# Edge products of a graph attention kernel multiplied by x over four PSUM banks: two operations of 2048 elements a tile in place of four of 1024, and the weighing in one operation

## The reference

```
w_m = (efeat @ W_msg + b_msg).reshape(E, in_f, -1)
w_a = (efeat @ W_attn + b_attn).reshape(E, in_f, -1)
h_src = feat[src][:, :, None]
e1 = w_m * h_src
e2 = w_a * h_src
seg_max = jax.ops.segment_max(e2, dst, num_segments=N)
ex = jnp.exp(e2 - seg_max[dst])
denom = jax.ops.segment_sum(ex, dst, num_segments=N)
attn = ex / denom[dst]
ft = jax.ops.segment_sum(e1 * attn, dst, num_segments=N)
return layernorm(x + ft.sum(axis=1))
```

## Time and profile before

| | us |
|---|---|
| runs of the kernel, median (3 runs) | 1687.11 |
| lowest and highest | 1686.28, 1688.92 |
| the profiled execution's own time | 1689.2 |
| its span in the profile | 1687.1 |
| busy: PE, VectorE | 1308.6, 1514.4 |
| busy: ACT, POOL | 987.8, 966.8 |

### The profile page before, as it was taken

The page is one execution under the profiler, slowest core; times in us unless marked ns, Lnnn a source line. Parts: engine busy times, 40 slices in busy tenths (PEclk is TensorE's granted clock), DMA queues, the critical chain, the costliest instruction groups (busy, mean ns, idle before and its releaser), DMA issues. The chain is left out here.

```text
span 1687.1 us, 20610 instructions
## 1 busy us (share of the span) xinstructions
PE 1308.6 (78%) x5657; PEld 675.5 (40%) x5657; DVE 1514.4 (90%) x1504; ACT 987.8 (59%) x2062; POOL 966.8 (57%) x878
## 2 busy tenths in 40 slices
PE   0002799999999999999999999999999999998300
PEld 0001444444444444444444444444444444443200
DVE  8623899999999999999999999999999999998368
ACT  1002567767767767777777677677676666664100
POOL 5777777777676767677677777676770000000170
PEclk9999899999999999999999999999999999999655
DMA  4314344444444444444444444444443223221250
GB/s 109 81 19 106 89 131 122 128 128 118 133 125 115 132 126 119 128 125 119 130 122 124 129 118 131 125 116 133 125 118 115 88 79 99 84 75 51 62 149 15
DMA packets 175870, 182.93 MB, mean 108 GB/s; under 512 B 48376, under 2 KB 131208, under 8 KB 175758
## 3 DMA queue, kind: packets, MB, share of 16 engines
q1 hardware_dynamic: 141838, 158.74, 30.0%
q0 software_dynamic: 33920, 22.89, 9.5%
HBM read 92.36 MB, written 89.41 MB: 108 GB/s over the span
## 5 line engine op out<-in xcount | busy, mean ns | idle before, releaser
L490 POOL DMA_INDIRECT split<-x_parts,edge_src x784 | 873.1, 1114 | 321.5 <-issue 221.6
L797 PE MATMUL bank_sum<-em,row_onehot 128*128 128x512 f32 x1760 | 861.6, 602 | 31.0 <-ACT sum_rows L661 31.0
L1031 DVE TENSOR_TENSOR em<-bank_prod,h_rows 128x1024 f32<-128x1024 f32 x440 | 515.7, 1213 | 41.8 <-issue 32.6
L797 PEld LDWEIGHTS bank_sum<-em,row_onehot 128*128 128x128 f32 x1760 | 307.5, 189 | 269.4 <-issue 235.2
L1049 DVE TENSOR_TENSOR em<-em 128x1024 f32<-128x1024 f32 x220 | 267.8, 1218 | 3.5 <-ACT em L620 3.5
L785 PE MATMUL bank_prod<-w_rows,partsT 100*128 100x512 bf16 x880 | 269.5, 388 | 1.5 <-DVE em L1031 1.5
L1074 DVE TENSOR_TENSOR em<-em,bank_max 128x2048 f32<-128x2048 f32 x110 | 250.7, 2279 | 3.2 <-ACT node_max L652 3.2
L661 ACT COPY sum_rows<-bank_sum 128x512 f32<-128x512 f32 x220 | 126.6, 576 | 176.6 <-PE bank_sum L797 176.6
L620 ACT ACTIVATE em<-em 128x2048 f32<-128x2048 f32 x110 | 210.5, 1913 | 1.5 <-DVE em L1074 1.4
L644 ACT COPY chunk_fwd<-bank_max 128x512 f32<-128x512 f32 x110 | 64.5, 586 | 238.0 <-PE bank_max L727 238.0
L490 POOL DMA_INDIRECT em<-sums,rec_from_i x4 | 4.0, 992 | 305.2 <-DMA sums<-sum_rows 304.3
(11 more groups left out here) (166 smaller groups left out, 1214.6 us busy)
## 6 DMA issues: line engine op xcount, KB each, us to landing
sums<-sum_rows SPq DMA_DIRECT2D x110, 512.0 KB, 3.0
rec<-split_records SPq DMA_DIRECT2D x220, 144.0 KB, 2.2
split_records<-split SPq DMA_DIRECT2D x97, 288.0 KB
mask<-tile_table SPq DMA_DIRECT2D x110, 192.0 KB, 3.3
split<-x_parts,edge_src POOLq DMA_INDIRECT x784
rel<-tile_table SPq DMA_DIRECT2D x110, 64.0 KB, 3.0
edge_feat<-in_features SPq DMA_DIRECT2D x97, 64.0 KB
flag<-tile_table SPq DMA_DIRECT2D x110, 2.0 KB
```

What stands on the lines that cost most here:

```text
L490: return nc.gpsimd.indirect_dma_start(out, None, src, bass.IndirectOffsetOnAxis(idx, 0))
L797: mm = nc.tensor.matmul(bank_sum[:, :], row_onehot[:, t % RING, g, :], em[:, t % RING, s * GROUPS + g, :, :, :].rearrange("p i m o -> p (i ...
L1031: V.tensor_tensor(em[:, v, 2 * j:2 * j + 2, :, :, :].rearrange("p s i m o -> p s i (m o)"), bank_prod[j % 2][:, :, :].rearrange("p s (i x) ...
```

## The change

The four PSUM banks of the products become one tensor, `bank_four`. `products` has two halves of four matmuls each in place of four pairs. Each half writes all four banks, and waits until the multiplication of the half before it has ended. `times_features` has two halves of 2048 elements. For that, `h_rows` is laid out by set and not by group, and ACT's copy writes it so. `weigh` takes all eight sets at once. The waits on `prod_ready`, `times_h` and `weighted` count accordingly.

```diff
-        h_rows = sb("h_rows", [P, 2, GROUPS, SLOTS * FEAT])
+        h_rows = sb("h_rows", [P, 2, SLOTS, GROUPS, FEAT])
...
-        bank_prod = [ps(f"bank_prod{i}", [P, 2, BOTH]) for i in range(2)]
+        bank_four = ps("bank_four", [P, 4, BOTH])
+        bank_prod = [bank_four[:, 0:2, :], bank_four[:, 2:4, :]]
...
-                since(act, times_h, 4 * (t - 1))
-                nc.scalar.copy(h_rows[:, t % 2, :, :].rearrange("p g k -> p (g k)"),
-                               bank_t[0][:, 0:GROUPS * SLOTS * FEAT]).then_inc(h_copied, 1)
+                since(act, times_h, 2 * (t - 1))
+                nc.scalar.copy(h_rows[:, t % 2, :, :, :].rearrange("p s g k -> p g s k"),
+                               bank_t[0][:, 0:GROUPS * SLOTS * FEAT].rearrange("p (g s k) -> p g s k", g=GROUPS, s=SLOTS)
+                               ).then_inc(h_copied, 1)
...
-                since(pe, times_h, 4 * t + j - 1)
-                for g in range(GROUPS):
-                    k = GROUPS * j + g
-                    mm = nc.tensor.matmul(bank_prod[j % 2][:, g, :], partsT[:, t % 2, k * P:(k + 1) * P],
+                since(pe, times_h, 2 * t + half)
+                for k in range(SIDE // 2):
+                    at = half * SIDE // 2 + k
+                    mm = nc.tensor.matmul(bank_four[:, k, :], partsT[:, t % 2, at * P:(at + 1) * P],
                                           w_rows[:, :], start=True, stop=True)
...
                 sum_slots(t - 2, 0, [0])
-                products(t + 1, 2)
                 give_features(t + 2)
-                products(t + 1, 3)
-                sum_slots(t - 2, 0, [1])
-                sum_slots(t - 2, 0, [2])
+                products(t + 1, 1)
+                sum_slots(t - 2, 0, [1, 2])
                 turn_back(t)
                 sum_slots(t - 2, 0, [3])
-                products(t + 2, 0)
                 pick_ends(t)
                 sum_slots(t - 2, 1, [0])
-                products(t + 2, 1)
+                products(t + 2, 0)
                 sum_slots(t - 2, 1, [1, 2, 3])
...
-                v_eng.wait_ge(prod_ready, 4 * t + j + 1)
-                h = h_rows[:, t % 2, :, FEAT * j:FEAT * (j + 1)]
-                V.tensor_tensor(em[:, v, 2 * j:2 * j + 2, :, :, :].rearrange("p s i m o -> p s i (m o)"),
-                                bank_prod[j % 2][:, :, :].rearrange("p s (i x) -> p s i x", i=FEAT),
-                                bc(h, 3, [P, GROUPS, FEAT, 2 * FEAT]), ALU.mult).then_inc(times_h, 1)
+                v_eng.wait_ge(prod_ready, 2 * t + half + 1)
+                h = h_rows[:, t % 2, 2 * half:2 * half + 2, :, :].rearrange("p s g k -> p (s g k)")
+                n = SIDE // 2 * FEAT
+                V.tensor_tensor(em[:, v, 4 * half:4 * half + 4, :, :, :].rearrange("p s i m o -> p (s i) (m o)"),
+                                bank_four[:, :, :].rearrange("p s (i x) -> p (s i) x", i=FEAT),
+                                bc(h, 2, [P, n, 2 * FEAT]), ALU.mult).then_inc(times_h, 1)
```

More of the change, by code:

```diff
@@ L422, in load_flags @@
                 since(sp, h_ready, t - 1)
-                since(sp, prod_ready, 4 * (t - 1))
+                since(sp, prod_ready, 2 * (t - 1))
                 sp.dma_start(flag8[:, w, :], tab_d[t:t + 1, 4 * WIDE:8 * WIDE].rearrange("t (k c) -> (t k) c", k=SIDE)
@@ L624, in copy_parts @@
                     return
-                since(act, prod_ready, 4 * (t - 1))
+                since(act, prod_ready, 2 * (t - 1))
                 for half in range(2):
@@ L774, in give_features, with products @@
                 mm.then_inc(h_ready, 1)
-            def products(t, j):
+            def products(t, half):
                 if not tile(t):
                     return
-                if j == 0:
+                if half == 0:
                     pe.wait_ge(t_copied, 2 * (t + 1))
                     pe.wait_ge(flags_landed[t % 2], 2 * rounds(t, 2))
-                since(pe, times_h, 4 * t + j - 1)
-                for g in range(GROUPS):
-                    k = GROUPS * j + g
-                    mm = nc.tensor.matmul(bank_prod[j % 2][:, g, :], partsT[:, t % 2, k * P:(k + 1) * P],
+                since(pe, times_h, 2 * t + half)
+                for k in range(SIDE // 2):
+                    at = half * SIDE // 2 + k
+                    mm = nc.tensor.matmul(bank_four[:, k, :], partsT[:, t % 2, at * P:(at + 1) * P],
                                           w_rows[:, :], start=True, stop=True)
@@ L792, in sum_slots @@
                 if slots[0] == 0:
-                    pe.wait_ge(weighted, 2 * (t + 1))
+                    pe.wait_ge(weighted, t + 1)
                     pe.wait_ge(onehot_ready, 2 * (t + 1))
@@ L1019, in _, with times_features @@
             v_eng.wait_ge(chunk_ready, 2)
-            def times_features(t, j):
+            def times_features(t, half):
                 if not tile(t):
@@ L1042, in run_forward, with weigh @@
                                      ALU.max).then_inc(fwd_done, 1)
-            def weigh(t, half):
+            def weigh(t):
                 if not tile(t):
@@ L1047, in weigh @@
                 v_eng.wait_ge(exp_done, t + 1)
-                m = em[:, t % RING, 4 * half:4 * half + 4, :, 1, :]
-                V.tensor_tensor(m, m, em[:, t % RING, 4 * half:4 * half + 4, :, 0, :], ALU.mult).then_inc(weighted, 1)
+                m = em[:, t % RING, :, :, 1, :]
+                V.tensor_tensor(m, m, em[:, t % RING, :, :, 0, :], ALU.mult).then_inc(weighted, 1)
             def max_slots(t):
@@ L1054, in max_slots @@
                 v = t % RING
-                v_eng.wait_ge(times_h, 4 * (t + 1))
+                v_eng.wait_ge(times_h, 2 * (t + 1))
                 V.tensor_tensor(max4[:, :, :, :], em[:, v, 0:4, :, 0, :], em[:, v, 4:8, :, 0, :],
@@ L1078, in _ @@
                 times_features(t + 1, 0)
+                run_forward(t)
+                weigh(t - 1)
                 times_features(t + 1, 1)
[L1080 to L1083, removed]
                 max_slots(t + 1)
-                weigh(t - 1, 1)
                 max_chunks(t + 1)
```

## The result

| | us |
|---|---|
| the changed kernel, median (4 runs) | 1779.15 |
| lowest and highest | 1777.65, 1779.79 |
| the kernel before beside it, median (4 runs) | 1687.94 |
| span in the profile, changed and before | 1777.2, 1687.1 |

The ratio is 1.054, with a 95% interval from 1.0522 to 1.0558: slower by 91 us, where 96.4 us were worked out. The time was forecast as 1784, within 1768 to 1802.

A forecast was written before the change was run, and what follows sets the result against it. A ring of PE and ACT was taken to bound the kernel, not VectorE. 104 x 0.87 = 90.5, plus 5.5 and 0.4, made 96.4 us: 1785.6 from the profiled run, about 1784 against the median, range 1768 to 1802.

The forecast's parts named there:

- the ring of PE and ACT: Steady iterations: PE and ACT alternately set the pace in four stretches, 3.12 + 2.49 + 3.01 + 3.95 = 12.57 us.
- VectorE's slack: In the changed kernel's iteration VectorE has about 1.3 us to spare and nobody waits for it.
- The term that carries the sum: Two more pairs of products stand in PE's own stretches: 0.87 us per iteration, 90.5 us over 104 iterations.
- Idle times: PE's waits for ACT's copies: 1.1 to 1.3 us before `give_features`, 0.7 to 0.85 before the second group's first sum.
- The first iterations: Five iterations before 221.98 us: 0.87 to 1.74 us each, 4.4 to 8.7 in all, put at 5.5.
- the steady part: From 221.98 to 1529.01 us, 104 iterations: 90.5 us more, within 83 to 100.
- the end: After 1529.01 us one group of products is left, costing 0.4 us.
- The saving on VectorE: Three merged pairs of operations save 0.08 us each, 0.24 us per iteration; none of it reaches the end.
- VectorE as the bound: Rival: VectorE sets the period, so the change gains 26 us, 1661 us, or 1670 counting only multiplication slots; 5%.
- One pair only: Rival: only one of two pairs loses its cover behind ACT, 0.43 us per iteration, about 1737 us; 5%.
- A slow multiplication over four banks: Rival: VectorE's four-bank multiplication is much slower than 2.28 us; at twice that, about 2115 us; 4%.
- A lower clock: Rival: PE, idle for longer, gets a lower clock; at half throughout, some 760 us more; 2%.

The follow-up runs named there:

- e1_order_only: The kernel before with only PE's order changed: third pair of products behind the source features, next tile's first pair behind the second group's first sum; 1780.23 us.
- e4_vector_more: The changed kernel with one more VectorE operation of 1024 elements per iteration, on data nobody uses; 1780.66 us.
- e13_before_covered: The kernel before with PE's fourth pair of products ahead of the source features, next tile's second pair ahead of the second group's first sum; 1649.43 us.
- e2_first_only: The kernel before with only the third pair of products moved behind the source features; 1732.81 us.
- e3_weigh_only: The kernel before with the weighing in one operation of 2048 elements, in place of the first of its two; 1687.07 us against 1687.26 before.
- e8_both_back_dve: The changed kernel with both halves of products in ACT's stretches and VectorE's second multiplication ahead of the weighing; 1656.78 us.
- e14_covered_weigh: The kernel before with PE's two open pairs of products moved into ACT's stretches and the weighing in one operation; 1651.01 us.
- e15_not_interleaved: The kernel before with PE's two open pairs moved into ACT's stretches, both weighings first, then the two maxima steps one behind the other; 1658.48 us.

## Why the prediction was right

- **Who sets the period.** Right: the ring of PE and ACT. e1_order_only reproduces the loss with the old banks, e4_vector_more shows VectorE's slack by filling it, and e13_before_covered shows that the same was true of the kernel before.
- **The term that carries the sum.** 0.87 us per iteration were worked out and 0.86 measured (13.43 less 12.57); over 104 iterations 90.5 and 89.6. e2_first_only shows that the first of its two parts is half of it.
- **Idle times.** The one before the source features is 1.09 us (1.1 to 1.3 were forecast). That before the sum of the second group is 0.60, below the 0.7 to 0.85 forecast. Its stretch kept its length; the four matmuls of `pick_ends` ahead of it, with 1.11 us in their row in e1_order_only and in the changed kernel against 1.03 in e2_first_only, hold some of the wait, and the page of the changed kernel has PEld L739 idle for L646.
- **The first iterations.** Mis-sized: 5.5 us forecast, 0.8 measured (222.78 against 221.98). That is 4.7 of the 6.3 us between the 96.4 forecast and the 90.1 that the span grew; the steady part has 0.9 of them and the end the rest. Even the 0.8 is nothing but the first iteration at the steady cost, since one iteration earlier the two kernels were level. The first multiplications of iteration 3, before and changed:

```profile
209.42 2.35 DVE L1031 TENSOR_TENSOR em<-bank_prod,h_rows 128x1024 f32<-128x1024 f32 x2 [0.96 <-issue]
```

```profile
209.36 2.29 DVE L1031 TENSOR_TENSOR em<-bank_four,h_rows 128x2048 f32<-128x2048 f32 x1 [1.57 <-issue]
```

The changed kernel's loop had started 0.83 us later (its first matmul at 149.94 against 149.11) and had caught up. In these iterations PE waits for loads and for VectorE, so a moved pair finds waits that are there anyway: in iteration 0 the source features waited 2.94 us for the DMA of `partsT` before, and 0.72 us for ACT after. That this is all of it is not shown; between 180 and 200 us the granted clock was 0.68 and 0.67 in the profile of the kernel before, and 1.00 in that of the changed one.
- **The saving on VectorE.** Wrong in size, without effect on the sum. The prediction had 0.24 us per iteration for three merged pairs, from slots of the merged operations alone. In the changed kernel the slot of the second multiplication is 2.32 us (752.02 to 754.34), since the maxima read what it wrote, and that of L1056 1.26. Together with 2.21, 2.19 and the rest the chain comes to 12.31 us where the prediction had 12.1; in the kernel before it was 12.25 (the period of e13_before_covered, which has the same operations). The step that failed was to count each operation's own slot and not the neighbour that it gets. VectorE's share is 92.2% for that reason, and not about 90. The slack came out near its forecast (1.1 against 1.3 us) partly by luck: the 0.24 us were not there, but the idle time of 0.23 us in the row also understates the slack before, 12.57 less 12.25, by 0.09 us.
- **The rivals.** VectorE as the bound: refuted by e4_vector_more for the changed kernel and by e13_before_covered for the one before; e3_weigh_only does not bear on it. One pair only: that is e2_first_only, 1732.81 us where 1737 was worked out, and it is not what the change does. A slow multiplication over four banks: 2287 ns on the page, no. A lower clock: 1.00 in both stretches of the steady part, no.

The Trainium skill, "Perfetto Trace Analysis", section "Identifying the Most-Contended Engine", points at the engine with the highest occupancy. That was VectorE with 98.23%, and it was not the bound; in e13_before_covered, at 99.99%, it was. In e8_both_back_dve, at 99.68%, it was not alone. The same page's section on "Optimizing Tensor Performance" asks to rotate independent matmul groups through PSUM banks, so that emptying one overlaps the next group's matmuls. The case agrees: giving that up makes PE wait 0.53 us in e8_both_back_dve, and after the preparation has ended the period stays at 12.26 us where two sets of banks reach 11.9.

## What to carry to other kernels

Two engines that are each 90% busy or more can both be waiting on a third. Compare the period of two stretches in which the busiest engine has different amounts of work: where the period stays, that engine does not set it. Then see which work stands inside the waits for the third engine, for it is free there and costs its full time everywhere else. Before merging operations, write down where the work that feeds them has to stand in the other engine's order, and whether the merged operation still separates two steps that depend on each other. When two orders are changed with the data layout, time the order alone: here it was the whole loss, and turned the other way the whole gain.

## What the runs showed of the hardware

On VectorE, an operation that reads the result of the one just before it, and waits for its semaphore, started about 0.11 us later than one that does not (1.25 us from start to start at 1024 elements against 1.14, in e14_covered_weigh and e15_not_interleaved against the kernel before; 2.32 against 2.20 at 2048 in the changed kernel). That is more than merging two operations of 1024 elements into one of 2048 saves (2 x 1.14 less 2.20, 0.08 us). No run tells the reading from the waiting. Reads over four PSUM banks ran at the same pace as over one (2.28 us for 2048 elements both times, L1031 and L1074 of the changed kernel).
